# A fused state-space and mixture-of-experts layer: a rearranged lead-in and another hand-written order of the engines' work

## What is computed

```python
x = x + mamba(layernorm(x))      # selective state space
x = x + moe(layernorm(x))        # 8 experts, the best 2 per token

# mamba, per sequence: d_inner 256, d_state 16, dt_rank 8
xi, res = split(x @ W_in)                       # 128 -> 2 x 256
u = silu(causal_conv4(xi) + conv_b)
delta_r, B, C = split(u @ W_x)                  # 8, 16, 16
delta = softplus(delta_r @ W_dt + b_dt)
h_t = exp(delta_t * A) * h_(t-1) + delta_t * B_t * u_t      # 16 states of 256 channels
y = (sum over states of h * C + u * D) * silu(res)
out = y @ W_out

# moe: scores = x @ gate_w.T; softmax of the two best scores gives cw
y = sum over e of cw[:, e] * (silu(x @ w1[e].T) @ w2[e].T)   # 128 -> 256 -> 128
```

## Time and profile before

| | |
|---|---|
| runs of the kernel | 1097.61, 1098.42, 1099.79 us (median 1098.42) |
| the profiled execution | 1100.4 us, span from the first to the last instruction 1098.4 us |
| mean granted TensorE clock over the span | 0.974 of full speed |
| busy share of the span | TensorE 95%, weight loads 69%, VectorE 93%, ScalarE 83%, GpSimd 88% |
| moved by DMA | 84.12 MB, mean 77 GB/s |
| scans | 256, 2275 ns each; products ahead of them 256, 1213 ns each |
| outputs on GpSimd | 256, 2366 ns each |

### The profile page before, as it was taken

One profiled execution on the slowest core, in us unless ns is written; L12 is line 12 of the kernel. 1 busy time (PEld: TensorE's weight loads), 2 busy tenths in 40 slices (PEclk: granted clock), 3 DMA queues, 4 the chain that ended last, 5 costly groups with the idle time before them and its releaser, 6 DMA issues.

```text
span 1098.4 us, 18682 instructions
## 1 busy us (share of the span) xinstructions
PE 1042.4 (95%) x6139; PEld 758.1 (69%) x6139; DVE 1016.4 (93%) x1051; ACT 907.8 (83%) x1381; POOL 961.4 (88%) x892
## 2 busy tenths in 40 slices
PE   6697879999999999999999999999999999989997
PEld 3455556777677777777777777777777776767775
DVE  4999999999999999999999999999999999999721
ACT  2988876988999898898999899899989989875533
POOL 3588876998999999999999999999999999799834
PEclk9598989999999999999999999999999999989999
DMA  4431222123031312204031320403131120320000
GB/s 149 178 135 39 77 77 79 58 79 106 0 135 51 126 59 89 95 0 160 24 125 58 109 74 26 158 0 125 58 135 39 68 105 0 135 87 11 11 10 10
DMA packets 37348, 84.12 MB, mean 77 GB/s; under 512 B 3304, under 2 KB 28192, under 8 KB 28960
## 3 DMA queue, kind: packets, MB, share of 16 engines
q1 hardware_dynamic: 36864, 83.06, 21.0%
q10 hardware_dynamic: 416, 0.30, 0.1%
HBM read 78.63 MB, written 4.72 MB: 76 GB/s over the span
## 4 chain that ended last, share of the span: by engine, by line
PE 74%; DVE 8%; issue 7%; ACT 6%; POOL 4%; DMA 0%; POOLq 0%; ACTq 0%; DVEq 0%
PE work L1781 17%; PE work L1771 16%; PE y_ps L1723 16%; PE work L1647 8%; DVE h L1245 6%; PE rows L1702 4%; PE work L1744 2%; ACT dA L856 2%; PE work L1631 2%; PE work L1666 2%; PE rows L1781 2%; POOL h L535 2%; PE work L1657 2%; PE rows L1771 1%; DVE rows L1235 1%
## 5 line engine op out<-in xcount | busy, mean ns | idle before, releaser
L535 POOL TENSOR_TENSOR h<-h,c_rows 128x1024 f32<-128x1024 f32 x256 | 600.3, 2366 | 55.3 <-DVE h L1245 55.2
L1245 DVE TENSOR_TENSOR_SCAN h<-dA,rows 128x1024 f32<-128x1024 f32 x256 | 579.0, 2275 | 1.1
L856 ACT ACTIVATE dA<-delta,a_neg 128x510 f32<-128x510 f32 x512 | 325.7, 707 | 8.3 <-issue 3.9
L1235 DVE TENSOR_TENSOR rows<-du,rows 128x1024 f32<-128x1024 f32 x256 | 306.7, 1213 | 4.3 <-PE rows L1702 4.2
L1723 PEld LDWEIGHTS y_ps<-ident,h 128*128 128x128 f32 x2048 | 241.9, 144 | 63.0 <-issue 34.7
L1723 PE MATMUL y_ps<-ident,h 128*128 128x128 f32 x2048 | 270.8, 279 | 10.9 <-POOL h L535 10.9
L1781 PEld LDWEIGHTS work<-w,hid 128*128 128x128 f32 x1856 | 223.1, 193 | 36.1 <-ACT hid L890 20.4
L1771 PE MATMUL work<-x2T,w 128*128 128x512 f32 x474 | 240.3, 602 | 2.9 <-ACT u L774 2.3
L1781 PE MATMUL work<-w,hid 128*128 128x128 f32 x1856 | 228.8, 277 | 4.0 <-ACT hid L890 3.8
L890 ACT ACTIVATE hid<-work 128x512 f32<-128x512 f32 x237 | 138.9, 596 | 64.6 <-PE work L1771 63.2
L575 POOL TENSOR_TENSOR x<-x,weighted 128x512 f32<-128x512 f32 x128 | 163.3, 1276 | 21.5 <-DVE weighted L1314 21.1
(11 more groups left out here) (142 smaller groups left out, 966.1 us busy)
## 6 DMA issues: line engine op xcount, KB each, us to landing
c_rows<-c_dram SPq DMA_DIRECT2D x64, 1024.0 KB, 4.9
x_in<-in_x SPq DMA_DIRECT2D x16, 256.0 KB, 2.9
x_again<-in_x SPq DMA_DIRECT2D x16, 256.0 KB, 3.4
out<-x SPq DMA_DIRECT2D x16, 256.0 KB, 2.6
w<-in_w1T SPq DMA_DIRECT2D x1, 1024.0 KB, 4.8
w<-in_w2T SPq DMA_DIRECT2D x1, 1024.0 KB, 7.0
h<-in_conv_w SPq DMA_DIRECT2D x1, 512.0 KB, 4.9
c_dram<-bcd SPq DMA_DIRECT2D x16, 32.0 KB, 1.6
```

Source lines behind the costliest of these rows:

```text
L535: nc.gpsimd.tensor_tensor(at, at, c_rows[:, n, :].unsqueeze(1).broadcast_to([P, H, T]), ALU.mult).then_inc(c_used, 1)
L856: last = nc.scalar.activation(two_seqs(dA[:, n % RING, half, :])[:, :, 1:], two_seqs(delta[:, half, :])[:, :, 1:], ACT.Exp, scale=a_neg[:, ...
L1235: nc.vector.tensor_tensor(rows[:, n % 2], du[:, j.odd], rows[:, n % 2, H - 1, :].unsqueeze(1).broadcast_to([P, H, T]), ALU.mult).then_inc( ...
L1245: nc.vector.tensor_tensor_scan(h[:, n % RING].rearrange("p h t -> p (h t)"), dA[:, n % RING].rearrange("p h t -> p (h t)"), rows[:, n % 2] ...
```

## The change

The lead-in: GpSimd does the power ahead of the copies of W_x, and the copies wait for the normalisation (`lead_norm`). `weigh_taps` is on VectorE for both halves, the second one behind the normalisation. TensorE turns a constant 30 times, and twice four times more: behind `turn_x(lead)` and behind the product for B, C and delta. The parts `middle` and `low` of round 0 are made by VectorE (in `first_delta`), and ScalarE does abs, exp and log of one half before those of the other. `skip(r[0])` comes behind eleven decays. `project_gate(r[0], 0)` comes ahead of the first `row_b`.

All lists have another order: the written-out first rounds and end as well as `round_`. The loop is also cut at another place: on TensorE ahead of `sum_states(6)`, on ScalarE between `decay(13)` and `low`, on VectorE ahead of `inputs(0)`, on GpSimd ahead of `outputs(4)`. No operation is added or left out but for the warm-up turns. One entry of `HIDDEN` and most of `MOVED` change. x is fetched two rounds ahead, not three.

```diff
-HIDDEN = ("hidden", ((0, 1), (0, 1), (1, 0), (0, 0), (1, 0), (0, 1), (0, 0), (1, 0)))
+HIDDEN = ("hidden", ((0, 1), (0, 1), (1, 0), (0, 0), (1, 0), (0, 1), (0, 0), (0, 1)))
...
-        WARM = 27
+        WARM = 30
...
# SP
             def round_(i):
-                three, four, five, seven = (i.later(-k) for k in (3, 4, 5, 7))
-                load_again(five)
-                load_c(four, 2)
-                store_c(three)
-                store_out(seven)
-                load_c(four, 3)
-                load_c(three, 0)
-                load_c(three, 1)
+                one, two, five = (i.later(-k) for k in (1, 2, 5))
+                load_c(two, 0)
                 load_x(i)
+                load_c(two, 1)
+                load_c(two, 2)
+                load_again(two)
+                store_c(one)
+                store_out(five)
+                load_c(two, 3)
...
# GpSimd, lead-in
             pool.wait_ge(constants_ready, CONSTANTS)
+            pool.wait_ge(variance_ready[0], 1)
+            nc.gpsimd.tensor_tensor(rstd[:, 0, :], variance[:, 0, :], power[:, 0:TB],
+                                    ALU.pow).then_inc(variance_ready[0], 1)
+            pool.wait_ge(lead_norm, 1)
             pool.wait_ge(w_x_loaded, 16)
...
-            pool.wait_ge(variance_ready[0], 1)
-            nc.gpsimd.tensor_tensor(rstd[:, 0, :], variance[:, 0, :], power[:, 0:TB],
-                                    ALU.pow).then_inc(variance_ready[0], 1)
-            pool.wait_ge(taps_loaded, 16 * TAP_LOADS)
-            weigh_taps(nc.gpsimd, 1)
...
# GpSimd, round_, the new order whole
+                add_expert(five, 0)
+                outputs(three, 4)
+                outputs(three, 5)
+                outputs(three, 6)
+                add_expert(five, 1)
+                add_expert(five, 2)
+                outputs(three, 7)
+                outputs(three, 8)
+                inverse_deviation(four, 1)
+                outputs(three, 9)
+                outputs(three, 10)
+                add_expert(five, 3)
+                outputs(three, 11)
                 add_soft(two)
+                outputs(three, 12)
+                add_expert(five, 4)
                 times_u(two)
                 outputs(three, 13)
+                add_expert(five, 5)
                 outputs(three, 14)
                 gap(four)
                 outputs(three, 15)
+                add_expert(five, 6)
+                routing(four)
                 outputs(two, 0)
                 outputs(two, 1)
                 outputs(two, 2)
-                add_expert(five, 6)
-                routing(four)
+                inverse_deviation(i, 0)
                 add_expert(five, 7)
                 outputs(two, 3)
...
# ScalarE, round_ (the first eleven calls, decay 8 to decay 13, stand at the end now)
                 hidden(four, 5, 1)
+                post_norm(three)
+                hidden(four, 6, 0)
                 pre_norm(i)
-                hidden(four, 6, 0)
-                post_norm(three)
                 hidden(four, 6, 1)
                 copy_x2T(three)
-                copy_xnT(i)
-                skip(one)
                 hidden(four, 7, 0)
                 hidden(four, 7, 1)
+                copy_xnT(i)
...
                 conv_silu(i, 0)
+                skip(one)
                 conv_silu(i, 1)
                 ratio_exp(three)
...
# ScalarE, first rounds
                 decay(r[1], 7)
+                copy_y(r[0])
                 decay(r[1], 8)
                 decay(r[1], 9)
-                copy_y(r[0])
...
# VectorE, first rounds
+            inputs(r[1], 1)
             scan(r[1], 0)
-            inputs(r[1], 1)
+            scan(r[1], 1)
             inputs(r[1], 2)
-            scan(r[1], 1)
+            inputs(r[1], 3)
             scan(r[1], 2)
-            inputs(r[1], 3)
+            gating(r[0])
+            scan(r[1], 3)
             inputs(r[1], 4)
-            scan(r[1], 3)
-            gating(r[0])
...
# TensorE, round_ (the calls from project_out to delta_rank(one, 0) stand at the end now)
                 sum_states(two, 7)
                 expert(four, 3, ...)
+                expert(four, 4, ...)
+                hidden(four, 5, 0, ...)
+                row_b(two, 12)
                 sum_states(two, 8)
-                expert(four, 4, ...)
-                row_b(two, 12)
-                hidden(four, 5, 0, ...)
                 sum_states(two, 9)
...
                 sum_states(two, 12)
+                expert(four, 6, ...)
                 row_b(one, 0)
-                expert(four, 6, ...)
                 convolve(i, 0, ...)
+                row_b(one, 1)
+                convolve(i, 1, ...)
+                expert(four, 7, ...)
+                row_b(one, 2)
                 sum_states(two, 13)
-                row_b(one, 1)
-                convolve(i, 1, ...)
-                row_b(one, 2)
-                expert(four, 7, ...)
                 sum_states(two, 14)
...
                 sum_states(one, 0)
                 sum_states(one, 1)
-                sum_states(one, 2)
                 row_b(one, 5)
                 expert(three, 0, ...)
                 hidden(three, 2, 0, ...)
                 row_b(one, 6)
                 hidden(three, 2, 1, ...)
+                sum_states(one, 2)
                 expert(three, 1, ...)
```

More of the change, by code:

```diff
@@ new lines, in _ @@
+            outputs(r[2], 13)
+            add_expert(r[0], 5)
+            outputs(r[2], 14)
+            gap(r[1])
+            outputs(r[2], 15)
+            add_expert(r[0], 6)
+            routing(r[1])
+            outputs(r[3], 0)
+            outputs(r[3], 1)
+            outputs(r[3], 2)
+            inverse_deviation(r[5], 0)
+            add_expert(r[0], 7)
+            outputs(r[3], 3)
+            run(pool, round_, 6, 5, 17)
+            add_expert(r[12], 0)
+            outputs(r[14], 4)
@@ L700, in _ @@
             outputs(r[15], 10)
+            add_expert(r[13], 5)
             outputs(r[15], 11)
[L702 to L704 removed]
             outputs(r[15], 12)
@@ L893, in round_ @@
                 one, two, three, four = (i.later(-k) for k in (1, 2, 3, 4))
-                decay(two, 8)
-                decay(two, 9)
-                hidden(four, 2, 0)
-                hidden(four, 2, 1)
-                decay(two, 10)
-                decay(two, 11)
-                high(one)
-                copy_bcd(one)
-                decay(two, 12)
-                middle(one)
-                decay(two, 13)
                 low(one)
@@ L944, in round_ @@
                 decay(one, 7)
+                decay(one, 8)
+                decay(one, 9)
+                hidden(three, 2, 0)
+                hidden(three, 2, 1)
+                decay(one, 10)
+                decay(one, 11)
+                high(i)
+                copy_bcd(i)
+                decay(one, 12)
+                middle(i)
+                decay(one, 13)
             def lead_in():
@@ L972, in lead_in @@
                                          scale=-1.0).then_inc((lead_exp, soft_exp)[half], 1)
-                middle(lead)
-                for half in range(H):
                     act.wait_ge((lead_exp, soft_exp)[half], 1)
@@ L977, in lead_in @@
                                          bias=1.0).then_inc((lead_log, soft_ready)[half], 1)
-                low(lead)
             lead_in()
-            skip(r[0])
             decay(r[0], 0)
             decay(r[0], 1)
+            decay(r[0], 2)
             pre_norm(r[1])
-            decay(r[0], 2)
             decay(r[0], 3)
@@ L993, in _ @@
             decay(r[0], 10)
+            skip(r[0])
             decay(r[0], 11)
+            decay(r[0], 12)
             gate_silu(r[0], 0)
@@ L1319, in round_ @@
                 three, four, five, six = (i.later(-k) for k in (3, 4, 5, 6))
-                inputs(four, 14)
-                scan(four, 13)
-                scan(four, 14)
-                top_two(five)
-                inputs(four, 15)
                 inputs(three, 0)
-                scan(four, 15)
-                weight_expert(six, 6)
+                inputs(three, 1)
                 scan(three, 0)
-                inputs(three, 1)
                 scan(three, 1)
@@ L1364, in round_ @@
                 weight_expert(five, 5)
+                inputs(three, 14)
+                scan(three, 13)
+                scan(three, 14)
+                top_two(four)
+                inputs(three, 15)
+                scan(three, 15)
+                weight_expert(five, 6)
             def split_dt_weights():
@@ L1822, in round_ @@
                 one, two, three, four = (i.later(-k) for k in (1, 2, 3, 4))
-                project_out(three, use_expert(four, 2), use_expert(four, 1), use_hid(four, 2, 0), use_gated(three))
-                row_b(two, 9)
-                hidden(four, 3, 0, use_low(one), use_hid(four, 2, 1))
-                sum_states(two, 5)
```

(14 more changed lines are left out.)

751 lines of the change are left out of this document (385 added, 366 removed).

## The result

The changed kernel took 1117.97 us (median; 1117.38 to 1118.24), the kernel before 1099.11 in the same session: an estimated ratio of 1.0166, 95% interval 1.0145 to 1.0187 (the two medians alone give 1.0172). The forecast was 1090.6 (1085.5 to 1098.5). The profiled execution took 1117.38, its span is 1115.3.

A forecast was written before the change was run, and what follows sets the result against it. TensorE's instruction list sets the round's 62.8 us, VectorE nearly full; gains come only from idle or half-clock time. Terms -3.3 - 2 - 1.5 - 1 = -7.8 us, from median 1098.42 to 1090.6 us (range 1085.5 to 1098.5).

The forecast's parts named there:

- Middle: Equal rounds: ScalarE's moved cut recovers about 2 of 2.9 us, GpSimd waits slightly; -1.5 us, bounds -2.9 and +4.
- the rivals: Four: new order returns half the gain (0.18); clock still falls, or taps' load binds lead-in (together 0.09); GpSimd late (0.11).
- Rival 3: Middle rounds: GpSimd too late once a round, at sum 1 behind routing; slower, 1102.9 us in its example; chance 0.11.
- Lead-in: Start to first convolutions: earlier start 2.2, full clock 1.7, less 0.4 for VectorE's copies; -3.3 us, bounds -0.9 and -4.5.
- the power may have to wait: Lead-in: GpSimd's power held by VectorE's first tap multiplication, to 7.3 to 8.3 us; convolutions start 2.2 us earlier, not 3.2.
- Opening: 27 to 165 us: gating wait of 1.2 us goes, first-round work fills TensorE's idle time; -2 us, bounds +3 and -5.
- bounds +3: Opening's worst case: new waits of about half the old ones, making it 3 us slower.
- Passage to the end: After the loop: expert 7 and row 2 ahead of sum 13 shorten TensorE's wait; -1 us, bounds -2 and +2.

The follow-up runs named there:

- experiment 1: Changed kernel with TensorE's loop cut moved back ahead of project_out, order of instructions unchanged: 1093.36 us, 0.9935 of the kernel before.
- experiment 8: Kernel before with 42 fulfilled waits more on ScalarE, so that its loop starts at 468 as in the changed kernel: 1098.82 us, 0.9989.
- experiment 9: Kernel before with the new lead-in alone and ScalarE's loop shifted, all round orders as before: 1094.27 us, 0.9948.
- 11: Changed kernel with TensorE's cut back ahead of project_out and round 0's skip back in its old place: 1093.28 us, 0.9935.
- 12: New lead-in, the kernel before's opening up to round 4's first convolution, then the changed order with TensorE's cut back ahead of project_out: 1093.66 us, 0.9932.
- 2: Changed kernel, cut left where the change put it, TensorE's loop shifted 102 slots by fulfilled waits: 1092.99 us, 0.994 of the kernel before.
- 7: Changed kernel with TensorE's rounds 5 to 15 written out in place of its hardware loop: 1093.24 us, 0.9936 of the kernel before.
- experiment 4: Kernel before with only TensorE's cut moved to ahead of sum 6, its own order kept: 1117.63 us, 1.0154.
- experiment 6: Changed kernel with TensorE's cut back ahead of project_out and its loop shifted by waits to start at slot 2957: 1124.05 us, 1.022.
- experiment 3: Kernel before with 87 more wait instructions on TensorE, so that its loop starts at slot 2957: 1133.29 us, 1.0304.

## Why the prediction was wrong

The prediction was wrong in its mechanism, and the step that failed is in **Middle**: "The loop's cut moves: on ScalarE it is now between decay 13 and low". It priced ScalarE's jump alone. TensorE's cut had moved too, and I gave it no price, though the rows had shown on ScalarE that an engine can wait for instructions at its jump. On TensorE the jump had cost nothing, because its loop was still held, and I read that as a property of the loop rather than of its place in the code. None of the rivals had it. Rival 3 came out on the right side (slower, once a round, at a state sum, with GpSimd as the page's releaser), but its mechanism is refuted: with the loop held and GpSimd's order unchanged (experiment 1), TensorE is busy for 500.00 of the 500 us from 400 to 900.

What the other terms came to: 1099.9 (before) - 1.1 (ScalarE's loop held) - 4.5 (lead-in) - 0.9 (all orders together) = 1093.4, and 24.6 for four jumps makes 1118. Each term is the difference of two runs that follow each other, so that they add up proves nothing; -1.1 is hardly clear of the noise and -0.9 within it.

- **Lead-in**, -3.3: -4.5 (experiments 8, 9). The start at 10.1 to 11.1 in all runs with it is as forecast, so is 7 us for sixteen convolutions. In the changed kernel's trace VectorE's first product ahead of a scan comes 4.2 us earlier (28.11 against 32.30): 2.8 of it by the earlier start, taken as 2.2 because "the power may have to wait", which it didn't; 1.5 by the convolutions, taken as 1.7; and measured from the copy of bcd it comes 0.2 us later, not 0.4. The exclusive lock of the Trainium skill (SBUF — State Buffer, "SBUF: two separate sides"), which I had weighed against the edit, is not seen between the power and the taps, though each reads two operands from SBUF: they start at 6.43 and 6.53 and take 1.04 and 1.08 us, against 1.03 and 1.10 before, and the measurement decides. It does fit the shift, which took 1.48 us beside GpSimd's multiplication and takes 0.15 with nothing beside it. Beside the second tap multiplication (8.24) the six copies of W_x take longer, 2.16 us against 1.48.
- **Opening**, -2: no gain. Against experiment 9, which has the old orders, TensorE in experiment 1 takes 2.5 us more from the first convolution to that of round 5 (260.7 against 258.2, within "bounds +3"), 1.1 less from there to that of round 15, and 2.1 less to the end. At these places VectorE is one scan further, so the opening loses less than the 2.5. The new order took round 0's skip behind eleven decays, a wait of 4.1 us; but neither its old place (11) nor the whole old opening (12) made the kernel faster. Where the opening's gain is lost stays open.
- **Middle**, -1.5: -2.5 over the ten rounds from the convolution of round 5 to that of round 15 (628.4 us in experiment 1, 630.9 before), some 1.4 of it by ScalarE's loop (629.6 in experiment 8). GpSimd's routing does wait for the ratio, 10.9 us in eight in experiment 1 (1.4 us each, not 0.1 to 0.5), and no sum on TensorE waits behind it.
- **Passage to the end**, -1: the last expert starts at 1084.99 in experiment 1, not 1083.7. From the convolution of the last round to the end it is 191.9 us against 193.0 in the profile before and 193.9 in experiment 9. Less of it is won than that seems: the last scan ends at the same time in experiments 9 and 1, and from there to the end it is 63.0 and 62.3 us. In these two traces that is all that the new orders win. The last scan in experiment 9, then in experiment 1:

```profile
1027.24 2.29 DVE L1244 TENSOR_TENSOR_SCAN h<-dA,rows 128x1024 f32<-128x1024 f32 x1
...
1027.34 2.28 DVE L1277 TENSOR_TENSOR_SCAN h<-dA,rows 128x1024 f32<-128x1024 f32 x1
```

Without TensorE's jumps the time would have been 1093.4 against 1090.6 forecast, inside the range. Experiments 1, 2 and 7 are 0.6% faster than before; each beats both kernels, and which of them is best can't be told.

A jump's price is the stop and the half clock behind it. The stops last 3.5 to 3.7 us in the changed kernel, 2.9 to 3.4 in experiment 4, 4.9 to 5.6 in experiment 6 and 5.5 to 5.9 in experiment 3. The clock stays at its lower level for about 3 us at two of the changed kernel's jumps and for nearly 7 at the other two, which is why these cost 1 us more; at the third jump of experiment 4 it did not fall, and the round took 66.4 us instead of 68.5 to 69.5. The first two windows are of the changed kernel, the third of experiment 4:

```profile
438.40:441.80 3.40, 3.24 (x10) 2.44 (x11) 0.55 (x1) 0.00 (x0) 3.11 (x8) 0.50 0.68 275
568.20:574.90 6.70, 5.69 (x14) 3.35 (x15) 1.64 (x1) 0.87 (x2) 6.17 (x13) 0.50 0.45 159
702.00:710.00 8.00, 7.51 (x41) 5.06 (x42) 5.02 (x8) 4.45 (x7) 4.36 (x3) 1.00 0.30 119
```

Open: why a stop is longer ahead of project_out than ahead of sum 6. The transfers of C run there: the DMA engines are busy for 0.82 to 1.03 of the stops of experiments 3 and 6 and for 0.14 to 0.23 of those of the changed kernel. That fits a fetch that has to share them, but in experiment 4 the share is 0.50 to 0.63 with the shortest stops of all, and no run moved the transfers. The first stop of the changed kernel, then of experiment 3:

```profile
434.82:438.56 3.74, 0.01 (x1) 0.00 (x1) 3.74 (x7) 1.46 (x3) 3.74 (x3) 0.98 0.20 53
432.80:438.30 5.50, 0.02 (x1) 0.00 (x0) 1.84 (x2) 3.53 (x5) 5.50 (x3) 0.71 1.03 393
```

## What to carry to other kernels

A hardware loop that nearly fills what an engine holds of its code can fall out of it by a shift of a few dozen instructions ahead of it: look at the instruction queues in the page's table of DMA queues, in the loop's stretch, before any reading of waits there, and distrust a releaser that ended long before. The remedy is cheap: move the cut, pad with fulfilled waits, or write the loop out. A reordered schedule is to be timed with the loop held on both sides, or the comparison is one of code placement.

## What had not been expected of the hardware

- The bound is sharp and comes back: loops of 1637 to 1639 slots starting at 2870, 2891, 2892 and 2918 are held, at 2935, 2956 and 2957 not, at 3058 again. That fits seven blocks of 256 slots held beside the one read ahead, with some 37 to 53 slots ahead of the program (my estimate from TensorE's starts). Nine packets a jump (eight blocks and the one read ahead) make the 36.
- ScalarE follows the same pattern in packets of 8 KB: a loop of 297 instructions starting at 447 is fetched again (20 packets more, five a jump), at 466 and 468 it is held.
- The stop is only part of a jump's price: with it the clock falls to its lower level, for about 3 or nearly 7 us, at all but one of the sixteen jumps seen.
- The profile calls the same stop by two names: "issue" with the cut ahead of project_out, and ahead of sum 6, which waits on GpSimd's semaphore too, mostly GpSimd's output (in experiment 4 "issue" in two of the four).
